# Routing block of a graph network with a mixture of experts: SyncE waits for the scatters and requests the first experts' rows

## The reference

```
x = x + gnn(layernorm(x), conv_weights, attn_l, attn_r, h_bias, src, dst, edge_type)   # 3750 nodes, 120000 edges
x = x + ffn(layernorm(x))

def ffn(x):                        # 3750 tokens of 256, 8 experts, 2 of them for each token
    logits = x @ Wr + br
    top_p, top_idx = top_k(softmax(logits), 2)
    weights = top_p / top_p.sum()
    xe = layernorm(x) * ln_g[e] + ln_b[e]
    y[e] = gelu(xe @ W1[e] + b1[e], exact) @ W2[e] + b2[e]     # 256 -> 1024 -> 256
    out = sum over the two chosen experts of weight * y[e]
```

## Time and profile before

| | us |
|---|---|
| median of 3 runs | 2166.85 |
| the runs | 2165.66 to 2166.98 |
| profiled execution, its own time | 2166.39 |
| span of its profile (first to last instruction) | 2164.6 |
| routing block, released to released | 1557.5 to 1675.7 |
| expert block, from its release on | 1675.7 to 2164.5 |

### The profile page before, as it was taken

The page is one execution under the profiler, slowest core; times in us unless marked ns, Lnnn a source line. Parts: engine busy times, 40 slices in busy tenths (PEclk is TensorE's granted clock), DMA queues, the critical chain, the costliest instruction groups (busy, mean ns, idle before and its releaser), DMA issues. The chain is left out here.

```text
span 2164.6 us, 38636 instructions
## 1 busy us (share of the span) xinstructions
PE 1834.3 (85%) x9042; PEld 1543.0 (71%) x9043; DVE 1152.1 (53%) x3072; ACT 851.3 (39%) x2220; POOL 1140.3 (53%) x1130
## 2 busy tenths in 40 slices
PE   7999878888888888888888888888552999999998
PEld 6788666666667676676766766666352888888887
DVE  7323146767767667767776676776773121212121
ACT  2222444544544444544544544542084222222222
POOL 4000277777777777777777777776055122222222
PEclk9999857888888888987887888887755999999999
DMA  6453344444444444444444444443144777776774
GB/s 242 158 198 143 140 110 109 113 113 110 112 113 110 112 111 111 112 112 110 112 112 110 112 112 110 112 108 91 55 160 142 240 224 231 219 223 221 231 215 130
DMA packets 119910, 308.99 MB, mean 143 GB/s; under 512 B 26919, under 2 KB 70823, under 8 KB 105668
## 3 DMA queue, kind: packets, MB, share of 16 engines
q0 software_dynamic: 60192, 149.24, 26.9%
q1 hardware_dynamic: 59556, 158.18, 21.1%
HBM read 250.66 MB, written 57.71 MB: 142 GB/s over the span
## 5 line engine op out<-in xcount | busy, mean ns | idle before, releaser
L744 POOL DMA_INDIRECT gath<-feats,idxT x996 | 951.9, 956 | 504.9 <-issue 293.8
L1042 PE MATMUL psP<-gath,hot 128*128 128x260 f32 x1992 | 612.1, 461 | 53.6 <-DVE gath L853 53.3
L1042 PEld LDWEIGHTS psP<-gath,hot 128*128 128x128 f32 x1992 | 431.3, 228 | 137.5 <-issue 50.1
L1029 PEld LDWEIGHTS psE<-er,hotT 128*128 128x128 f32 x1992 | 292.2, 225 | 124.0 <-issue 123.3
L1029 PE MATMUL psE<-er,hotT 128*128 x1992 | 306.9, 303 | 80.7 <-issue 38.3
L965 ACT COPY hotT<-psOT 128x512 f32<-128x512 f32 x249 | 145.1, 583 | 450.6 <-PE psOT L1013 449.5
L955 ACT ACTIVATE hot<-cst,ndlT 128x128 f32<-128x128 f32 x996 | 317.4, 393 | 4.7 <-PEq L312 4.7
L862 DVE TENSOR_TENSOR acc<-acc,psP 128x260 f32 x498 | 210.6, 423 | 195.7 <-PE psP L1042 76.1
L1564 POOL DMA_INDIRECT out<-yrow,node x66 | 102.6, 1554 | 391.8 <-DVE yrow L1679 296.4
L853 DVE TENSOR_TENSOR gath<-gath,psA 128x1024 f32<-128x1024 f32 x249 | 301.2, 1220 | 9.9 <-ACT gath L985 2.5
L1634 ACT ACTIVATE hT<-psH,w1buf 128x256 f32<-128x256 f32 (+1 forms) x320 | 119.3, 435 | 352.3 <-PE psH L1594 352.3
(11 more groups left out here) (226 smaller groups left out, 1192.4 us busy)
## 6 DMA issues: line engine op xcount, KB each, us to landing
w1buf<-in_experts SPq DMA_DIRECT2D x40, 1030.0 KB, 7.8
w2buf<-in_experts SPq DMA_DIRECT2D x40, 1024.0 KB, 5.7
feats<-frow SPq DMA_DIRECT2D x29, 1040.0 KB, 3.9
gath<-feats,idxT POOLq DMA_INDIRECT x996
meta<-in_edges SPq DMA_DIRECT2D x464, 12.0 KB
xrow<-slots_x SPq DMA_DIRECT2D x26, 258.0 KB, 6.5
b_all<-in_b SPq DMA_DIRECT2D x40, 128.0 KB, 6.4
xs<-xb SPq DMA_DIRECT2D x5, 768.0 KB, 9.9
```

The costliest lines, as they stand in the source:

```text
L744: pool.indirect_dma_start(gath[:, r, u], None, feats, bass.IndirectOffsetOnAxis(ap=idxT[:, r, u:u + 1], axis=0)).then_inc(gath_in[r], 16)
L1029: ins = pe.matmul(psE[:, u * W % 512:u * W % 512 + W], hotT[:, j % 2, k * P:(k + 1) * P], tables[k // BLK], start=True, stop=True)
L1042: ins = pe.matmul(psP[:, bank(g, b, r), 0:FW], hot[:, r, u], gath[:, r, u], start=u % BLK == 0, stop=u % BLK == BLK - 1)
```

## The change

In the routing block GpSimd no longer waits for its scatters. SP does, after its waits for pads and stores, and then requests the rows of steps 0 and 1, still within the routing's block. The two requests leave the head of the expert block. For this `xrow` and its two semaphores become tensors of the whole program; they are allocated ahead of the routing's own. The rows are the same, into the same two buffers, with the same semaphores counting.

```
 sp, routing block:
                 load_weights(sp, sb, 0, experts1, experts2, b2)
                 sp.wait_ge(pads_in, 16 * E)
                 sp.wait_ge(out_stored, 16 * (NB + 1))
+                sp.wait_ge(scattered, 32 * TILES)
+                load_first_rows(sp, sb, slots_x)
 gpsimd, routing block:
                                                 xn[:, n, k], None).then_inc(scattered, 16)
-                pool.wait_ge(scattered, 32 * TILES)
+def load_first_rows(sp, sb, slots_x):
+    for n in range(2):
+        at = sp.value_load(sb["row_of"][0:1, n:n + 1], min_val=0, max_val=SLOTS - SLOT_TILE)
+        sp.dma_start(sb["xrow"][:, n], slots_x[bass.ds(at, SLOT_TILE), :].rearrange("(j p) f -> p j f", p=P)).then_inc(
+            sb["x_in"][n], 16)
 sp, expert block:
-                load_rows(Step(None, 0))
-                load_rows(Step(None, 1))
                 load_weights(sp, sb, 1, experts1, experts2, b2)
 build:
+        sb["xrow"] = keep("xrow", [P, 2, SLOT_TILE // P, DW])
+        sb["x_in"] = [ctx.enter_context(nc.semaphore(f"x_in{q}")) for q in range(2)]
```

More of the change, by code:

```diff
@@ L1433, in expert_stage @@
         w1buf, w2buf, b2_all = sb["w1buf"], sb["w2buf"], sb["b2_all"]
-        xrow = t("xrow", [P, 2, HALVES, DW])
+        xrow, x_in = sb["xrow"], sb["x_in"]
         node = t("node", [P, RING, HALVES, 1], I32)
@@ L1443, in expert_stage @@
         w1_in, w2_in = sb["w1_in"], sb["w2_in"]
-        x_in = [sem("x_in0"), sem("x_in1")]
         y_added = [sem("y_added0"), sem("y_added1")]
```

## The result

| | before | changed |
|---|---|---|
| median of 20 runs | 2169.82 | 2165.09 |
| the runs | 2165.66 to 2174.62 | 2160.82 to 2168.59 |
| span of the profile | 2164.6 | 2163.4 |

The ratio of the two is 0.9981, 95% interval 0.9974 to 0.9987: **4.1 us less**, between 2.8 and 5.6, where 3.8 were forecast (the medians themselves are 4.7 us apart). The time itself, 2165.09, lies above the range, because the kernel before takes 2169.82 over 20 runs and not the 2166.5 from which I counted.

The account below looks back on a forecast made before the run. The chain from last scatter landing through GpSimd's drain, release and row request to rows bounds the first layer. Moving it from 1681.78 to 1677.95 gains 3.8 us; from 2166.5 that gives 2162.7 us, range 2160.4 to 2164.8.

Parts of the forecast that it names:

- The base: Starting time of the kernel before: 2166.5 us, the average of four known executions, from which the gain was subtracted.
- the clock: PE's rise from 1.2 to 2.4 GHz in the first layer: 1 to 2 us earlier or later shifts time 0.5 to 1.0.
- What bounds the kernel: Routing's end to first layer: last landing 1670.4, drain to 1675.5, release 1675.7, row request 1676.49, rows 1679.37; PE gapless from 1684.
- Part 1: Row requests ahead of the release: SP asks at 1671.2 and 1672.4, rows land 1674.1 and 1675.6, SP reports 1673.2.
- Part 2: GpSimd enters its DRAIN at routing's end without waiting for scatters; drain predicted to end at 1675.3 to 1675.5.
- the upper end: GpSimd's drain at routing's end waits for the landings, then takes its whole 4.96 us, ending at 1675.3 to 1675.5.
- below 1673.2: Sign at routing's end: GpSimd's DRAIN ending before this time, in us, would show case (a).
- (a): Rival at routing's end: GpSimd's drain doesn't wait for landings, over at 1671.4; gain 5.3 us, time 2161.2; chance 0.27.
- (b): Rival at routing's end: drain works while the last scatters land, ending between 1672 and 1675; gain 4.6 us; chance 0.10.
- the likeliest case: Routing's end: drain ends 1675.4, release 1675.6, PE begins 1675.7, first layer 1677.95; gain 3.8 us; chance 0.50.
- (d): Rival at routing's end: drain grows with transfers under way, 16 us for six; 7 us slower, 2173.6; chance 0.05.
- (c): Rival at the expert block's head: instruction supply or late clock comes last, release unmoved; gain 2.0 to 3.0 us; chance 0.08.

## Why the prediction was right or wrong

- **The base was wrong, and that put the time outside the range.** The step "the four executions known average 2166.5, and from there 3.8 us lead to 2162.7" took four executions that agree within 1.3 us for the kernel's time. Twenty runs, three of those four among them, spread over 9 us with a median of 2169.82, 3.3 above; from there 3.8 us lead to 2166.0, and 2165.09 was measured. Of the seventeen later runs only three are below 2167, as all four known ones were; whether that was luck or something that differed between then and later, the runs don't say. Much of such a spread shows at the edge stage's end, which moved by 7.8 us between profiles of this size, in a part that the change doesn't touch. The range held the unknown costs of the change and the clock, and nothing for the base; moved up with it, to 2163.7 to 2168.1, it would have held the result.
- **What bounds the kernel: right.** Landing, drain, release, request, rows was the chain; a gain ahead of the first layer reached the end.
- **Part 1, SP: right.** Requests 0.8 and 2.0 us behind the landing as computed; rows there 2.7 and 3.0 us after them (2.88 and 3.20 forecast); SP's report 2.5 us behind the landing (2.8 forecast). For another kind of chip it lacked a term: it took "the DMA engines are free by then" for given, and where SP is late the weights are in the way, at some 5 us.
- **Part 2, the drain: wrong.** "I take the upper end" rested on 5.4 and 5.5 us after the last data in two blocks. That agreement was a coincidence, since the two drains follow different distances. In all 18 profiles GpSimd's drain behind the gathers ends 7.9 us behind the last gather's issue (1504.64 to 1512.5 in rows 7 and 8), 6.9 behind the end of its record; behind scatters without a wait it ends 2.5 us behind the landing or 5.9 behind the issue. The term of 5.1 us from the landing to the drain's end was twice too long.
- **Which rival it was.** By the sign that I had set, a drain that ends within 2.8 us of the landing ("below 1673.2"), and by PE's reason, "rows", it is case (a), to which I gave 0.27. Its mechanism isn't that of (a), a drain that doesn't wait for the landings, but that of (b), a drain that goes through part of its work while they come in, to which I gave 0.10. By the profiles the change is worth 4.7 to 5.5 us, against the 3.8 of the likeliest case, 4.6 of (b) and 5.3 of (a). The interval of the first result, 2.8 to 5.6, holds them all: that the forecast gain of 3.8 lies near the measured 4.1 doesn't speak for the likeliest case.
- **The rule on records of the Trainium skill** ("Perfetto Trace Analysis", "DMA Instruction — SWDGE (GPSIMD)"): a record ends when the last descriptor is written, not when the data has moved. The trace of the changed kernel agrees: the record is 0.97 us long, and the landing comes 7.2 us after its start. That nothing is left for a DRAIN to wait for does not follow: it ended at 1678.0, 8.7 us after that record's end.
- **The clock: right as a spread.** It rose 1.3 us into the first layer instead of 2.8, worth 0.8 us here; over the other profiles 1.1 to 4.2 us.
- **(d), a drain that grows with the transfers under way:** didn't happen; six scatters were under way and it took 2.5 us behind the last. **(c):** nothing at the head of the expert block came late.

What stays open: why the edge stage takes some 383 us more on some chips, with SP's own instructions late there; what GpSimd does in the 2.5 us behind a landing; and why its drain takes 6.9 us from the last record behind the gathers, 4.96 behind the scatters and 3.03 at the kernel's end. None of this was tried.

## What to carry to other kernels

A wait that stands ahead of a block's end should be on the engine whose next work needs it, and not on GpSimd after software-made transfers: its DRAIN starts only behind that wait, and cost 5.1 us behind the landing instead of 2.5 here. Before a small transfer on the critical path is asked for earlier, look at what stands ahead of it in the queues; large weights that are needed later belong behind it, and those needed at once ahead of it. Take the base from as many runs as the difference wants: four executions within 0.06% missed a median by 0.15%.

## What the runs showed of the hardware

- GpSimd's DRAIN behind the scatters costs time of its own: 4.96 us with all of them landed, and without the wait its end is 5.9 us behind the last issue or 2.5 us behind the landing, whichever is later. Behind the gathers of the edge block it was 7.9 us behind the last issue in all 18 profiles, on both kinds of chip.
- The first two steps' rows, 258 KB each, asked for 1.7 us behind the second of 2 MB of weights, landed after 6.9 to 8.8 us in five profiles; asked for with no weights under way after 2.6 to 3.2 us. The last scatter landed after 2.8 us with no weights beside it, 4.5 and 6.2 with 1 MB, 6.7 to 7.4 with 2 MB.
- The changed kernel took 2165 us on some chips and 2568 to 2573 on others. Its gain of 0.2% on the one kind was absent on chip 15 (1.0006, 0.9987 to 1.0025); on chips 9 and 11 the intervals leave it open.
